# Second attention of an eight-stage network: projections as three float32r products of split operands, output weights reloaded per batch

## What is computed

```python
q = (x @ Wq.T).reshape(B, T, 16, 128)      # B=8, T=256, Wq/Wk/Wv are 2048 x 256
k = (x @ Wk.T).reshape(B, T, 16, 128)
v = (x @ Wv.T).reshape(B, T, 16, 128)
q, k = rmsnorm(q, gq), rmsnorm(k, gk)      # per head, over 128
attn = softmax(causal(q @ k.T * 128**-0.5))
out  = (attn @ v).reshape(B, T, 2048) @ Wo.T   # Wo is 256 x 2048
```

## Time and profile before

| | us |
|---|---|
| median of 3 runs | 3052.41 |
| lowest, highest | 3046.9, 3059.18 |
| the profiled execution's own time | 3054.93 |
| its span, first to last instruction | 3053.1 |
| second attention, first key group to last output matmul | about 795 of the span |

### The profile page before, as it was taken

The page is one execution under the profiler, slowest core; times in us unless marked ns, Lnnn a source line. Parts: engine busy times, 40 slices in busy tenths (PEclk is TensorE's granted clock), DMA queues, the critical chain, the costliest instruction groups (busy, mean ns, idle before and its releaser), DMA issues. The chain is left out here.

```text
span 3053.1 us, 42176 instructions
## 1 busy us (share of the span) xinstructions
PE 2563.8 (84%) x13936; PEld 1824.5 (60%) x13936; DVE 1842.7 (60%) x4199; ACT 1341.0 (44%) x3669; POOL 446.6 (15%) x392
## 2 busy tenths in 40 slices
PE   7988999979999999998698777766666665999997
PEld 5665544446665666567476656554444444877876
DVE  4665333355574556555555766667777775777777
ACT  5663455534453444434122132156676662333332
POOL 2441000000000000000121000036556550000000
PEclk9998999989999999999799988889888875999999
DMA  4002000000000000002000000010000003000000
GB/s 151 10 7 83 1 0 0 0 35 1 3 3 3 0 3 3 3 0 90 3 0 0 0 1 0 0 51 4 3 7 3 3 1 135 1 0 0 0 0 28
DMA packets 18735, 48.77 MB, mean 16 GB/s; under 512 B 3184, under 2 KB 15216, under 8 KB 17008
## 3 DMA queue, kind: packets, MB, share of 16 engines
q1 hardware_dynamic: 18672, 47.98, 4.1%
HBM read 39.59 MB, written 2.10 MB: 14 GB/s over the span
## 5 line engine op out<-in xcount | busy, mean ns | idle before, releaser
L1914 ACT ACTIVATE l3a_pr<-psum,l3a_nm 128x128 f32<-128x128 f32 (+1 forms) x512 | 205.8, 420 | 91.4 <-DVE l3a_nm L2020 91.4
L1235 POOL TENSOR_TENSOR l1f_acc<-l1f_t 128x512 f32<-128x512 f32 x4 | 6.3, 1573 | 1309.2 <-DVE l1f_t L1298 1309.2
L108 DVE TENSOR_TENSOR x_sb<-psum,x_sb 128x512 f32 (+2 forms) x48 | 41.6, 868 | 253.8 <-PE psum L950 135.5
L757 DVE TENSOR_TENSOR l0f_hg<-l0f_sq,psum 128x512 f32<-128x512 f32 x128 | 87.8, 688 | 151.1 <-ACT l0f_sq L689 148.4
L997 ACT ACTIVATE l1a_pr<-psum,l1a_nb,l1a_rq 128x128 f32<-128x128 f32 (+1 forms) x256 | 127.2, 509 | 87.7 <-DVE l1a_nb L1062 85.3
L2274 ACT ACTIVATE l3f_sg<-psum 128x512 f32<-128x512 f32 x96 | 57.3, 597 | 241.0 <-PE psum L2230 241.0
L2227 PE MATMUL psum<-l3f_x_hi,l3f_w_hi 128*128 x384 | 154.3, 402 | 6.9 <-DVE l3f_w_lo L2310 6.9
L1934 ACT ACTIVATE l3a_pr<-l3a_pr,l3a_nb,l3a_rec 128x128 f32<-128x128 f32 (+1 forms) x256 | 119.4, 542 | 79.5 <-DVE l3a_nb L2038 79.5
L2228 PE MATMUL psum<-xT,l3f_w_hi 128*128 x384 | 153.0, 398 | 0.0
L2229 PE MATMUL psum<-l3f_x_hi,l3f_w_lo 128*128 x384 | 152.2, 396 | 0.0
L1777 PE MATMUL psum<-cf_sb,l3a_pr 128*128 128x128 f32 x384 | 77.1, 323 | 81.9 <-ACT l3a_pr L1934 81.9
(11 more groups left out here) (423 smaller groups left out, 6934.6 us busy)
## 6 DMA issues: line engine op xcount, KB each, us to landing
w_l3f_all<-l3f_all_dram SPq DMA_DIRECT2D x1, 9216.0 KB, 25.2
w_l0f_w<-l0f_w_dram SPq DMA_DIRECT2D x2, 2048.0 KB, 10.0
w_l1f_all<-l1f_all_dram SPq DMA_DIRECT2D x1, 2560.0 KB, 8.7
x_sb<-x_dram SPq DMA_DIRECT2D x1, 2048.0 KB, 8.4
l0a_xc<-xT SPq DMA_DIRECT2D x8, 256.0 KB, 2.5
w_l1a_q<-l1a_q_dram SPq DMA_DIRECT2D x1, 2048.0 KB, 8.0
w_l1a_k<-l1a_k_dram SPq DMA_DIRECT2D x1, 2048.0 KB, 13.3
w_l1a_v<-l1a_v_dram SPq DMA_DIRECT2D x1, 2048.0 KB, 16.2
```

The source lines that it names most:

```text
L1914: last = nc.scalar.activation(pr[:, r, a, g, k], S[:, g, k], ACT.Exp, bias=nm[:, i % 2, g, t:t + 1], accum_out=sums[:, r, a, g, t:t + 1])
```

## The change

The raw query, key and value weights are split once, at the start of the stage: ACT writes `w_hi` (ten instructions of 128 x 2 x 512: keys 4, queries 4, values 2), DVE subtracts for the keys, POOL for queries and values. `w_lo` lies in place of the raw weights. Of the values only the column blocks 0 and 1 of each token tile (`VS = 2`) are split; blocks 2 and 3 stay float32. The batch's x is split by ACT and DVE: for the first batch ahead of the loop, for each later one at the end of the batch before it. SBUF room is made by sharing: `ksq` and `qsq` lie in `pr`, `qn` in `pt`, `xc` in a table that the first attention used, and `wo` in `kT`, so that the output weights are loaded again for each batch, in eight pieces of 256 KB, piece n once the scores of pair n are done.

```diff
@@
...
-        xc = sb("xc", [P, KD, T])
+        w["over_weights"]()
+        w_lo = {n: sb("w%s_lo" % n, [P, KD, H * HD], F32R) for n in "qkv"}
+        for n in ("gq", "gk"):
+            sb(n, [P, 1])
+        xc = c["l0_k"]
         qT = sb("qT", [HD, H, T])
         kT = sb("kT", [HD, H, T])
         va = sb("va", [P, TT, H * HD])
         ko = sb("ko", [P, H * T])
         kn = ko[:, :].rearrange("p (t h d) -> p (t h) d", t=TT, h=H)
         oT = ko[:, :].rearrange("p (h t) -> p h t", h=H)
-        ksq = sb("ksq", [P, 2, 512])
-        qsq = sb("qsq", [P, 2, 512])
-        qn = sb("qn", [P, 2, 512])
+        x_hi = sb("x_hi", [P, KD, T], F32R)
+        x_lo = sb("x_lo", [P, KD, T], F32R)
+        VS = 2
+        w_hi = {n: sb("w%s_hi" % n, [P, KD, m * 512], F32R) for n, m in (("k", 4), ("q", 4), ("v", VS))}
         pr = sb("pr", [P, 2, 2, 3 * P])
         pt = sb("pt", [P, 2, 2, 3 * P])
+        ksq = qsq = pr[:, :, :, :].rearrange("p a i k -> p (a i k)")[:, 0:1024].rearrange("p (a k) -> p a k", a=2)
+        qn = pt[:, :, :, :].rearrange("p a i k -> p (a i k)")[:, 0:1024].rearrange("p (a k) -> p a k", a=2)
...
@@
-        wo = sb("wo", [P, H, D])
+        wo = kT
...
@@
-                sp.dma_start(wo[:, :, :].rearrange("p h d -> p (h d)"), w["o_dram"]).then_inc(o_loaded, 16)
-                with sp.Fori(0, B) as b:
-                    sp.wait_ge(xc_free, b + 1)
-                    sp.dma_start(xc[:, :, :], xT[:, :, bass.ds(b * T, T)]).then_inc(x_staged, 16)
+                def load_output_weights(done):
+                    for n in range(NG):
+                        sp.wait_ge(s_ps, done + n + 1)
+                        sp.dma_start(wo[:, 2 * n:2 * n + 2, :].rearrange("p h d -> p (h d)"),
+                                     w["o_dram"][:, 2 * n * D:2 * (n + 1) * D]).then_inc(o_loaded, 16)
+
+                sp.wait_ge(xc_free, 1)
+                sp.dma_start(xc[:, :, :], xT[:, :, 0:T]).then_inc(x_staged, 16)
+                with sp.Fori(0, B - 1) as b:
+                    sp.wait_ge(xc_free, b + 2)
+                    sp.dma_start(xc[:, :, :], xT[:, :, bass.ds(b * T + T, T)]).then_inc(x_staged, 16)
+                    load_output_weights(b * NG)
+                sp.wait_ge(xc_free, B + 1)
+                sp.dma_start(xc[:, :, :], xT[:, :, 0:T]).then_inc(x_staged, 16)
+                load_output_weights((B - 1) * NG)
...
@@
                 with pe.Fori(0, B) as b:
-                    pe.wait_ge(x_staged, b * 16 + 16)
+                    pe.wait_ge(xlo_ready, b + 1)
+
+                    def project(out, n, t, cols):
+                        for k in range(KD):
+                            hi, lo = x_hi[:, k, t * P:(t + 1) * P], x_lo[:, k, t * P:(t + 1) * P]
+                            mm(out, hi, w_hi[n][:, k, cols], start=(k == 0), stop=False)
+                            mm(out, hi, w_lo[n][:, k, cols], start=False, stop=False)
+                            last = mm(out, lo, w_hi[n][:, k, cols], start=False, stop=(k == KD - 1))
+                        return last
 
                     def turn_queries(j):
                         pe.wait_ge(q_out, b * NJ + j + 1)
@@
                         t, cols = j // 4, slice((j % 4) * 512, (j % 4 + 1) * 512)
                         if j >= 2:
                             pe.wait_ge(k_out, b * NJ + j - 1)
-                        for k in range(KD):
-                            last = mm(bank(j % 2), xc[:, k, t * P:(t + 1) * P], w["k"][:, k, cols], start=(k == 0), stop=(k == KD - 1))
-                        last.then_inc(k_ps, 1)
+                        if j < 4:
+                            pe.wait_ge(klo_ready, j + 1)
+                        project(bank(j % 2), "k", t, cols).then_inc(k_ps, 1)
 
                     def turn_keys(m):
                         if m >= 2:
@@
                         t, cols = j // 4, slice((j % 4) * 512, (j % 4 + 1) * 512)
                         if j >= 2:
                             pe.wait_ge(q_out, b * NJ + j - 1)
-                        for k in range(KD):
-                            last = mm(bank(2 + j % 2), xc[:, k, t * P:(t + 1) * P], w["q"][:, k, cols], start=(k == 0), stop=(k == KD - 1))
-                        last.then_inc(q_ps, 1)
+                        if j < 4:
+                            pe.wait_ge(qvlo_ready, j + 1 + min(j + 1, VS))
+                        project(bank(2 + j % 2), "q", t, cols).then_inc(q_ps, 1)
                         if j >= 2:
                             pe.wait_ge(v_out, b * NJ + j - 1)
-                        for k in range(KD):
-                            last = mm(bank(6 + j % 2), xc[:, k, t * P:(t + 1) * P], w["v"][:, k, cols], start=(k == 0), stop=(k == KD - 1))
+                        if j % 4 < VS:
+                            last = project(bank(6 + j % 2), "v", t, cols)
+                        else:
+                            for k in range(KD):
+                                last = mm(bank(6 + j % 2), xc[:, k, t * P:(t + 1) * P], w["v"][:, k, cols], start=(k == 0), stop=(k == KD - 1))
                         last.then_inc(v_ps, 1)
                         if j >= 1:
                             turn_queries(j - 1)
@@
                     pe.wait_ge(o_ready, b * NG + NG)
-                    pe.wait_ge(o_loaded, 16)
+                    pe.wait_ge(o_loaded, b * NG * 16 + NG * 16)
@@
             @block.scalar
             def _(act):
                 nc.scalar.preload_act_table(ACT.Exp)
+
+                def split_x(done):
+                    act.wait_ge(x_staged, done * 16 + 16)
+                    nc.scalar.activation(x_hi[:, :, :], xc[:, :, :], ACT.Copy).then_inc(xhi_ready, 1)
+
+                split_x(0)
+                w["early"](act)
+                for names in ("k", "qv"):
+                    for m in range(4):
+                        for n in names if m < VS else names[0]:
+                            cols = slice(m * 512, (m + 1) * 512)
+                            nc.scalar.activation(w_hi[n][:, :, cols], w[n][:, :, cols], ACT.Copy).then_inc(whi_ready, 1)
                 with act.Fori(0, B) as b:
...
@@
                         if j >= 2:
                             act.wait_ge(qT_ps, b * NJ + j - 1)
                             act.wait_ge(q_sum, b * NJ + j - 1)
+                        else:
+                            act.wait_ge(k_sum, b * NJ + NJ)
                         nc.scalar.activation(qn[:, j % 2, :], bank(2 + j % 2), ACT.Copy)
                         nc.scalar.activation(qsq[:, j % 2, :], bank(2 + j % 2), ACT.Square).then_inc(q_out, 1)
                         if j >= 3:
@@
+                    split_x(b + 1)
+
+            @block.gpsimd
+            def _(pool):
+                for m in range(4):
+                    for i, n in enumerate("qv" if m < VS else "q"):
+                        cols = slice(m * 512, (m + 1) * 512)
+                        pool.wait_ge(whi_ready, 4 + m + min(m, VS) + i + 1)
+                        nc.gpsimd.tensor_tensor(w_lo[n][:, :, cols], w[n][:, :, cols], w_hi[n][:, :, cols].bitcast(F32),
+                                                ALU.subtract).then_inc(qvlo_ready, 1)
 
             @block.vector
             def _(dve):
                 st = Steps(dve, steps, L1A_STEPS)
                 w["early"](dve)
                 nc.vector.tensor_tensor(gain[:, :], w["gq"], w["gk"], ALU.mult)
+
+                def split_x(done):
+                    dve.wait_ge(xhi_ready, done + 1)
+                    nc.vector.tensor_tensor(x_lo[:, :, :], xc[:, :, :], x_hi[:, :, :].bitcast(F32), ALU.subtract).then_inc(xlo_ready, 1)
+
+                split_x(0)
+                for m in range(4):
+                    cols = slice(m * 512, (m + 1) * 512)
+                    dve.wait_ge(whi_ready, m + 1)
+                    nc.vector.tensor_tensor(w_lo["k"][:, :, cols], w["k"][:, :, cols], w_hi["k"][:, :, cols].bitcast(F32),
+                                            ALU.subtract).then_inc(klo_ready, 1)
                 with dve.Fori(0, B) as b:
@@
                             normalise(n - 1)
+                    split_x(b + 1)
                     dve.wait_ge(y_ps, b + 1)
@@
             if stage == "l1a":
+                waiting[stage][1]["over_weights"] = scopes[stage].close
                 waiting[stage][1]["o_dram"] = wts["l1a_o"]
```

More of the change, by code:

```diff
@@ L809, in l1_attention @@
         x_staged = sem("x_staged")
+        xhi_ready = sem("xhi_ready")
+        xlo_ready = sem("xlo_ready")
+        whi_ready = sem("whi_ready")
+        klo_ready = sem("klo_ready")
+        qvlo_ready = sem("qvlo_ready")
         xc_free = sem("xc_free")
```

## The result

| | before | after |
|---|---|---|
| median, us | 3050.47 (4 runs) | 2996.19 (4 runs) |
| lowest, highest | 3046.9, 3059.18 | 2994.62, 3000.96 |
| the profiled execution, its span | 3054.93, 3053.1 | 2994.62, 2992.8 |

The ratio is 0.9819, with a 95% interval of 0.9801 to 0.9838: 54 us faster, where 49 were predicted (2996 against 3003).

The account below looks back on a forecast made before the run. PE was taken to bound the projections, its saving moving everything behind it in all 8 batches. 45.1 + 0.1 + 4.0 = 49.2 us off the profiled 3054.93 gave 3005.7, as a median 3003, range 2997 to 3010.

Parts of the forecast that it names:

- A group of products: In projections, six float32r products at 0.2311 us take 1.387 instead of 1.717 us; 20 groups save 6.6 us per batch.
- The second rival: Products run at the pace of float32 passes, 0.2147 us each, about 1.7 us less per batch: 2990; chance 0.05.
- Keys with a faster PE: Eight key groups save 0.330 us each, less 0.17 us waiting for ACT to empty banks: net 2.47 us per batch.
- Queries and values: Twelve groups save 0.330 us each, with DVE's key scaling still done in time: net 3.97 us per batch.
- The start: Batch 0's keys: PE begins earlier, then idles 4.2 us behind ACT's weight conversions and meets low clock; net gain 0.1 us.
- POOL's price: Each of POOL's six weight subtractions at the stage's start takes 2.35 to 3.14 us, taken as 3.14; hidden.
- Sum: 45.1 us for batches 1 to 7, 0.1 for batch 0's keys, 4.0 for its queries and values: 49.2 us.
- Work with cover: Splitting the next x at a batch's end hides under PE's output work; uncovered, about 1.2 us per batch.
- the output weights: Eight 256 KB loads per batch land by 713.3, upper bound 719.0, before the output starts at 719.78: no cost.
- Start and handshake: Rival: POOL at twice its price (12 us once) or key waits for ACT (4.6 us): 3008 to 3020; chance 0.10.
- The slower case: Rival: products do not overlap, 0.39 us each, a group 2.36 us, 160 groups +103 us: 3155; chance 0.03.
- A saving taken back per batch: Rival: something called hidden, the late output weights above all, takes back PE's saving: about 3045; chance 0.02.

Follow-up runs that it names:

- The run with four products per group: Changed kernel without the product of x's low and the weights' high part: second attention 720.4 us (-44.5), a batch free of drops 86.2, run 2956.16.
- the run without cover: Changed kernel with DVE splitting the next x only after adding and measuring the output: second attention 799.4 us (+34.5).
- The bunched loads: Changed kernel with all eight output weight loads issued behind the batch's last pair of scores: second attention 766.7 us (+1.8).
- the 10.36 us: DVE's four key subtractions when POOL, not ACT, converts the changed kernel's query and value weights: second attention 761.6 us, run 2994.37, ratio 0.9813.

## Why the prediction was right

**What bounds the kernel.** Right. PE's saving moved everything behind it, in all batches.

**A group of products.** 0.2311 us apart forecast, 0.23 measured; six are 1.387 us. By the formula of the Trainium skill (TensorE: Matmul & The Clock Gate, "Back-to-back issue gap") they would be 215.8 ns apart. The formula names no type, and these float32r products don't follow it. The second rival, with nearly that pace, forecast a batch about 1.7 us shorter than the sum did, 90.5 us by estimate; it takes 92.2.

**Keys with a faster PE.** 11.27 us forecast, 11.26 measured; two groups 2.83 and 2.85. The run with four products per group shows what lies behind: there the handshake is longer than the group and sets the pace.

**Queries and values.** 32.09 us forecast (36.06 - 3.97), 32.06 measured. A batch free of drops went from 98.6 to 92.2 us, 6.4 against 6.44.

**The start.** The mechanism was right to the engine: PE idle between the second and third group, ended by ACT's square, then the lower clock again. The sizes were off and cancelled, which was luck. DVE's first piece came at 631.5 and not 629.0 (2.3 of these 2.5 us are the stage's later beginning in this profile); the first two groups took 5.5 us at the lower level and not 4.3; so the idle time was 2.67 us instead of 4.2. Together 0.45 us where 0.1 was forecast. POOL's price was 2.35 us, the lower bound, where I took 3.14: of the two rows the one with the same number of elements was the right one, not the one that I held to be nearer for its two full inputs. It made no difference, since POOL was under its cover.

**Sum.** From the profile: 0.45 for batch 0's keys, 5.15 for the rest of batch 0, 46.0 for batches 1 to 7, which is 51.6. Predicted 0.1, 4.0 and 45.1. The clock drops that the two profiles don't share make up most of the difference: before had one in batch 0 (1.0 us) and two later (1.6 each), after two of 0.8 and 1.0. Without them it is 0.45 + 4.15 + 44.6 = 49.2, and the sum was 49.2. That they agree to 0.1 us is again in part luck: 0.35 us too little for the start and 0.5 too much for batches 1 to 7. The 54 us of the medians have 3 more than the stage. The fourth attention's 14 us between executions is enough for that, but nothing shows where they come from.

**Work with cover, and the output weights.** Right that both cost nothing; the run without cover shows 4 to 6 us per batch for the split (I had said 1.2, a clear miss, though no term of the sum hung on it). The bunched loads cost about 0.2 us in all, so the upper bound, which allowed none, was nearly right.

**The rivals.** Start and handshake: the handshake cost 0.08 us per two groups, the start nothing. The slower case, products that don't overlap, fell with the first timeline. A saving taken back per batch did not occur.

## What to carry to other kernels

When PE is the bound, a matmul price read from rows elsewhere in the same kernel, times the count, plus one handshake per buffer, gave the saving of the stage to 5%. Work that is added at the start of a stage is worth an order: a conversion that nobody needs yet must not stand ahead of the evacuation that PE needs now. And before a gain under 10 us is looked for in this kernel's total, count the batches with a clock drop; the period free of drops shows 0.7 us where five whole runs show nothing.

## What the runs showed of the hardware

In these rows DVE and POOL exclude each other by whole instructions. I had quoted the Trainium skill (GPSIMD Engine Reference, "Specifications") that they contend, and had no price. The price is the rest of the other's instruction: a DVE instruction of 0.19 us took 2.27 beside a POOL subtraction of 2.44, and its end fell 0.05 us behind POOL's. In after one instance is there already: POOL's first piece takes 3.05 us instead of 2.35, and the 0.7 more is nearly the 0.8 us for which DVE's last key subtraction still ran. It hit DVE's subtractions, `TENSOR_SCALAR` and `SCALAR_TENSOR_TENSOR` between SBUF tiles; `TENSOR_REDUCE` at 646.83 kept its 0.69 us under the same POOL instruction. The Trainium skill (SBUF — State Buffer, "Who interferes with whom") says just this: a lock on a shared port pair, held for the whole instruction, which DVE needs for two inputs in SBUF and for some copies and `tensor_scalar`, and never for a reduction. These rows agree. With it, the 10.36 us could have been estimated beforehand: four DVE subtractions (4.88 us) taking turns with two POOL subtractions (4.70), one cast (1.04) and the rest of the first cast (0.65) give 11.3 us.
